# Two rearranged stages of a four-layer decoder kernel: the products of a memory chunk regrouped around their waits, and the quantized network's elementwise work cut into thirds and quarters

## The reference, cut to what matters

```python
# first branch: 4 chunks of 64 tokens, 8 batches, W1 and W2 of 32 x 32 each
for c0 in range(0, S, CHUNK):
    g = _grad_fn(W_state, k[:, sl], v[:, sl]) * GRAD_SCALE
    g = g * jnp.minimum(MAX_GRAD_NORM / gn, 1.0)             # gn: norm of g, per token
    # per token t:  Sm = eta*Sm - theta*g ;  Wm = (1-alpha)*Wm + Sm
    (S_state, W_state), Wtraj = jax.lax.scan(step, (S_state, W_state), xs)
    h = jax.nn.silu(jnp.einsum('btd,btod->bto', q[:, sl], W1t))   # W1t, W2t: the state at token t
    outs.append(jnp.einsum('bto,btpo->btp', h, W2t))
# last branch
def act_qdq(x):
    scale = jnp.maximum(jnp.max(jnp.abs(x)) / qmax, 1e-12)   # one step size for the whole tensor
    return jnp.clip(jnp.round(x / scale), -qmax - 1.0, qmax) * scale
x = act_qdq(x)
up = act_qdq(x @ lpbq_dequant(w_up).T)
gate = act_qdq(x @ lpbq_dequant(w_gate).T)
sig = fixed_qdq_u16(jax.nn.sigmoid(gate))
gate = act_qdq(gate * sig)
o = act_qdq(gate * up)
return o @ lpbq_dequant(w_down).T
```

## Time and profile before

| | us |
|---|---|
| median of three runs (lowest, highest) | 5105.78 (5103.46, 5122.11) |
| profiled execution | 5113.21 |
| its span, first to last instruction | 5111.4 |
| PE busy | 4084.8 (80%) |
| DVE busy | 3495.8 (68%) |
| ACT busy | 2508.5 (49%) |
| POOL busy | 1378.3 (27%) |

### The profile page before, as it was taken

How to read it: one execution, slowest core, us unless ns; L and a number is a source line. 1 busy time by engine, 2 the same in 40 slices (tenths; PEclk the granted TensorE clock), 3 DMA queues, 4 the chain that set the end, 5 groups by cost and what they waited for, 6 DMA issues and landing times. The chain is left out here.

```text
span 5111.4 us, 77588 instructions
## 1 busy us (share of the span) xinstructions
PE 4084.8 (80%) x29250; PEld 2216.5 (43%) x29315; DVE 3495.8 (68%) x5424; ACT 2508.5 (49%) x3542; POOL 1378.3 (27%) x1033
## 2 busy tenths in 40 slices
PE   5740596999999999999995995866995768888872
PEld 3530234666666666666652332432443332222221
DVE  5379444677777777777784445766773648888867
ACT  2120142666666666666662223543563345776762
POOL 0000300566666666666665302000000100000000
PEclk5565698999999999999997997987997788999986
DMA  0010001000000000000003106316540333323200
GB/s 19 1 60 0 0 0 51 1 14 1 14 1 14 14 1 14 1 14 1 1 1 129 58 0 148 54 14 108 81 72 4 95 66 59 55 43 49 47 2 8
DMA packets 135604, 167.70 MB, mean 33 GB/s; under 512 B 19499, under 2 KB 108093, under 8 KB 134677
## 3 DMA queue, kind: packets, MB, share of 16 engines
q1 hardware_dynamic: 127540, 146.39, 14.1%
q0 software_dynamic: 6528, 16.42, 1.3%
q10 hardware_dynamic: 1184, 0.12, 0.0%
HBM read 125.31 MB, written 34.55 MB: 31 GB/s over the span
## 5 line engine op out<-in xcount | busy, mean ns | idle before, releaser
L2992 POOL TENSOR_TENSOR arena<-arena 128x512 f32<-128x512 f32 (+1 forms) x768 | 1131.8, 1475 | 692.2 <-ACT arena L2948 638.8
L2443 ACT ACTIVATE arena<-ps 128x1024 f32<-128x1024 f32 (+1 forms) x688 | 703.9, 1024 | 331.9 <-PE ps L2368 321.4
L2461 DVE TENSOR_REDUCE arena<-ps 128x2 f32<-128x826 f32 (+1 forms) x576 | 565.0, 981 | 183.6 <-PE ps L2314 175.1
L3008 DVE TENSOR_TENSOR arena<-arena 128x1024 f32<-128x1024 f32 (+1 forms) x448 | 645.9, 1480 | 13.8 <-ACT arena L2975 13.8
L3030 DVE TENSOR_TENSOR arena<-ps,arena 128x512 f32<-128x512 f32 (+1 forms) x768 | 530.3, 691 | 177.8 <-ACT arena L2942 144.4
L2314 PE MATMUL ps<-arena 48*128 48x413 bf16 (+3 forms) x1920 | 435.2, 333 | 135.0 <-DVE arena L2461 67.2
L2942 ACT ACTIVATE arena<-ps 128x1024 f32<-128x1024 f32 (+1 forms) x448 | 410.6, 961 | 204.8 <-PE ps L2870 194.3
L2854 PE MATMUL ps<-arena 128*128 128x256 f32 (+1 forms) x1664 | 444.1, 392 | 20.5 <-DVE arena L3016 19.2
L2948 ACT ACTIVATE arena<-arena 128x1024 f32<-128x1024 f32 (+1 forms) x448 | 424.9, 992 | 50.7 <-DVE arena L3008 48.2
L2387 PE MATMUL ps<-arena 128*9 128x256 f32 (+2 forms) x5504 | 435.3, 388 | 11.7 <-ACT arena L2431 8.0
L2870 PE MATMUL ps<-arena 64*128 64x256 f32 (+1 forms) x3328 | 427.3, 391 | 5.6 <-ACT arena L2964 1.3
(11 more groups left out here) (645 smaller groups left out, 5796.0 us busy)
## 6 DMA issues: line engine op xcount, KB each, us to landing
arena<-ctx_parts SPq DMA_DIRECT2D x96, 200.1 KB
arena<-ctx_parts SPq DMA_DIRECT2D x192, 100.1 KB
arena<-in_ctx_feat SPq DMA_DIRECT2D x8, 1601.0 KB, 6.5
arena<-in_ctx SPq DMA_DIRECT2D x16, 768.0 KB
arena<-diff_att_stack SPq DMA_DIRECT2D x60, 192.0 KB
ctx_parts<-arena SPq DMA_DIRECT2D x24, 400.2 KB, 3.7
arena<-in_w SPq DMA_DIRECT2D x1, 6416.0 KB, 18.6
arena<-in_ctx_feat SPq DMA_DIRECT2D x8, 800.5 KB
```

What stands on the lines that cost most here:

```text
L2443: act.activation(self.prob[0:rows, u % 3, :], self.ps[0:rows, 2 * (u % 2):2 * (u % 2) + 2, :].rearrange("p n c -> p (n c)"), ACT.Exp).then ...
L2461: ins = dve.tensor_reduce(dst[:, :, j // 2], self.ps[:, 4:6, 0:hi - lo], AX.X, ALU.max)
L2992: pool.tensor_tensor(acc[0:rows, u % 2, :], before, sc[0:rows, u % 2, t, :], ALU.add).then_inc(added, 1)
L3008: dve.tensor_tensor(e, e, mb[0:rows, u % 2, None, :].to_broadcast([rows, n, 2 * S]), ALU.subtract).then_inc(sub_done, 1)
```

## The change

In a memory chunk, a product of one row of zeros (512 columns, bf16) now opens bank 6 and bank 0: it writes zeros over the whole bank, and all products after it only add. So the eight batches' products with `Wst` and `Sst` no longer have to stand next to the one with `cg`. They are issued ahead of the wait for `cg_ready`, and in the second sum behind a wait for `hA` and `hB` and ahead of the wait for the masked product. The update products move up, from the end of the chunk to just behind the first sum. VectorE's order in a chunk stays the same. A tile `zero` is cleared once.

In the quantized network `gate` is computed ahead of `up`. Magnitudes are taken part by part, each followed by a maximum over three columns. `to_grid` has two passes in place of three (no clipping), and the weights lose their clip. `gate`, the sigmoid, and the passes after it go by thirds of 2048 columns, and the last quantization by quarters of the tokens ([128, 3, 512]), each of which releases a quarter of the down products.

```diff
+            dve.memset(m["zero"][:, :], 0.0)
...
+            def open_bank(n):
+                pe.matmul(ps[0:HM, n, :], m["zero"][:, 0:HM], m["zero"][:, HM:], start=True, stop=False)
+            open_bank(6)
+            for b in range(B):
+                pe.matmul(bank(6)[:, b, :], m["Wst"][:, 0, b, :], qA[:, b, :], start=False, stop=False)
+                pe.matmul(bank(6)[:, b, :], m["Sst"][:, 0, b, :], qB[:, b, :], start=False, stop=False)
             pe.wait_ge(cg_ready, 1)
             for b in range(B):
-                pe.matmul(bank(6)[:, b, :], m["Wst"][:, 0, b, :], qA[:, b, :], start=True, stop=False)
-                pe.matmul(bank(6)[:, b, :], m["Sst"][:, 0, b, :], qB[:, b, :], start=False, stop=False)
-                ins = pe.matmul(bank(6)[:, b, :], cg[:, 1, b, :], GM[:, b, :], start=False, stop=True)
+                ins = pe.matmul(bank(6)[:, b, :], cg[:, 1, b, :], GM[:, b, :], start=False, stop=(b == B - 1))
             ins.then_inc(y_ready, 1)
...
+            pe.wait_ge(hab_ready, 1)
+            open_bank(0)
+            for b in range(B):
+                pe.matmul(bank(0)[:, b, :], m["Wst"][:, 1, b, :], hA[:, b, :], start=False, stop=False)
+                pe.matmul(bank(0)[:, b, :], m["Sst"][:, 1, b, :], hB[:, b, :], start=False, stop=False)
+            pe.wait_ge(gm2_ready, 1)
...
-            tt(hB[:, :, :], h[:, :, :], Bc, ALU.mult)
+            tt(hB[:, :, :], h[:, :, :], Bc, ALU.mult).then_inc(hab_ready, 1)
...
                 for c in range(4):
-                    ins = pe.matmul(ps[:, 4 * (n % 2) + c, :], wT[:, n * P:(n + 1) * P],
+                    k = (n + FT) % (2 * FT)
+                    ins = pe.matmul(ps[:, 4 * (n % 2) + c, :], wT[:, k * P:(k + 1) * P],
                                     xq[:, c * BANK:(c + 1) * BANK], start=True, stop=True)
                 ins.then_inc(s["part_in"], 1)
-            pe.wait_ge(s["o_ready"], 1)
             for t in range(NT):
+                if t % 4 == 0:
+                    pe.wait_ge(s["o_ready"], t // 4 + 1)
...
-            act.wait_ge(s["sig_in"], 1)
-            act.activation(sig[:, :, :], gate[:, :, :], ACT.Sigmoid).then_inc(s["sig_ready"], 1)
+            for f in range(FT):
+                act.wait_ge(s["sig_in"], f + 1)
+                act.activation(sig[:, f, :], gate[:, f, :], ACT.Sigmoid).then_inc(s["sig_ready"], 1)
...
+            def part_magnitude(n, f, t):
+                return dve.tensor_reduce(part_mag[:, n - 1, f:f + 1], t, AX.X, ALU.max, apply_absolute_value=True)
...
+            def to_grid(n, t, out):
+
                 link(ts(out, t, grid[:, 1, n:n + 1], ROUND, ALU.mult, ALU.add))
-                link(ts(out, out, -ROUND, QMAX, ALU.add, ALU.min))
-                link(ts(out, out, -QMAX - 1.0, grid[:, 0, n:n + 1], ALU.max, ALU.mult))
-
-            magnitude(0, x_tok[:, :, :].rearrange("p t d -> p (t d)"), AX.X)
+                return ts(out, out, -ROUND, grid[:, 0, n:n + 1], ALU.add, ALU.mult)
...
-            link(ts(wt[:, :], wt[:, :], 7.0, -8.0, ALU.min, ALU.max))
...
+            for f in range(FT):
+                dve.wait_ge(s["part_out"], f + 1)
+                ins = part_magnitude(1, f, gate[:, f, :])
+            magnitude_of_parts(1, ins)
+            dve.wait_ge(s["part_out"], FT + 1)
+            part_magnitude(2, 0, up[:, 0, :])
+            step_of(1)
+            for f in range(FT):
+                to_grid(1, gate[:, f, :], gate[:, f, :]).then_inc(s["sig_in"], 1)
+            for f in range(1, FT):
+                dve.wait_ge(s["part_out"], FT + f + 1)
+                ins = part_magnitude(2, f, up[:, f, :])
+            magnitude_of_parts(2, ins)
...
+            step_of(2)
             flat = lambda t: t[:, :, :].rearrange("p f t -> p (f t)")
...
+            link(to_grid(2, flat(up), flat(up)))
+            step_of(3)
+            for f in range(FT):
+                link(to_grid(3, gate[:, f, :], gate[:, f, :]))
+                link(tt(up[:, f, :], up[:, f, :], gate[:, f, :], ALU.mult))
+                ins = part_magnitude(4, f, up[:, f, :])
+            magnitude_of_parts(4, ins)
+            step_of(4)
+            for g in range(4):
+                cut = up[:, :, g * BANK:(g + 1) * BANK]
+                to_grid(4, cut, cut).then_inc(s["o_ready"], 1)
```

More of the change, by code:

```diff
@@ L590, in _ @@
                 ins.then_inc(upd_ready, 1)
+            pe.wait_ge(h_ready, 1)
+            for b in range(B):
+                ins = pe.matmul(bank(7, 64)[:, b, :], h0[:, b, :], h[:, b, :], start=True, stop=True)
+            ins.then_inc(g2_ready, 1)
+            pe.wait_ge(hab_ready, 1)
+            open_bank(0)
+            for b in range(B):
+                pe.matmul(bank(0)[:, b, :], m["Wst"][:, 1, b, :], hA[:, b, :], start=False, stop=False)
+                pe.matmul(bank(0)[:, b, :], m["Sst"][:, 1, b, :], hB[:, b, :], start=False, stop=False)
+            pe.wait_ge(gm2_ready, 1)
+            for b in range(B):
+                ins = pe.matmul(bank(0)[:, b, :], cg[:, 0, b, :], GM2[:, b, :], start=False, stop=(b == B - 1))
+            ins.then_inc(out_ready, 1)
         @block.scalar
@@ L747, in stage0 @@
         m["W2"] = st.sb("W2", [HM, B, HM])
+        m["zero"] = st.sb("zero", [1, HM + BANK], BF16)
         memory_inputs(env, m)
@@ L4374, in _ @@
-            dve.wait_ge(s["part_out"], 2 * FT)
-            magnitude(2, gate[:, :, :], AX.XY)
-            flat = lambda t: t[:, :, :].rearrange("p f t -> p (f t)")
-            to_grid(2, flat(gate), flat(gate))
-            dve.sem_inc(s["sig_in"], 1)
-            to_grid(1, flat(up), flat(up))
-            dve.wait_ge(s["sig_ready"], 1)
-            link(ts(flat(sig), flat(sig), 65536.0, ROUND, ALU.mult, ALU.add))
-            link(ts(flat(sig), flat(sig), -ROUND, 65535.0, ALU.add, ALU.min))
@@ L4384, in _ @@
-            link(stt(out=flat(gate), in0=flat(sig), scalar=1.0 / 65536.0, in1=flat(gate), op0=ALU.mult, op1=ALU.mult))
-            magnitude(3, gate[:, :, :], AX.XY)
-            to_grid(3, flat(gate), flat(gate))
-            link(tt(flat(up), flat(up), flat(gate), ALU.mult))
-            magnitude(4, up[:, :, :], AX.XY)
-            to_grid(4, flat(up), flat(up))
-            dve.sem_inc(s["o_ready"], 1)
+            for f in range(FT):
+                dve.wait_ge(s["part_out"], f + 1)
+                ins = part_magnitude(1, f, gate[:, f, :])
@@ new lines, in _ @@
+            magnitude_of_parts(1, ins)
[9 more added lines that the diff above has]
+            for f in range(FT):
+                dve.wait_ge(s["sig_ready"], f + 1)
+                link(ts(sig[:, f, :], sig[:, f, :], 65536.0, ROUND, ALU.mult, ALU.add))
+                link(ts(sig[:, f, :], sig[:, f, :], -ROUND, 65535.0, ALU.add, ALU.min))
+                link(stt(out=gate[:, f, :], in0=sig[:, f, :], scalar=1.0 / 65536.0, in1=gate[:, f, :], op0=ALU.mult,
+                         op1=ALU.mult))
+                ins = part_magnitude(3, f, gate[:, f, :])
@@ new lines, in _ @@
+            magnitude_of_parts(3, ins)
+            step_of(2)
+            flat = lambda t: t[:, :, :].rearrange("p f t -> p (f t)")
+            link(to_grid(2, flat(up), flat(up)))
+            step_of(3)
+            for f in range(FT):
+                link(to_grid(3, gate[:, f, :], gate[:, f, :]))
[3 more added lines that the diff above has]
+            step_of(4)
```

32 lines of the change are left out of this document (13 added, 19 removed).

## The result

The changed kernel takes 5064.43 us, the median of seven runs (5046.86 to 5068.68). The kernel before, run beside it, has a median of 5105.78 us (seven runs, 5088.74 to 5122.23). The ratio over all the runs is 0.9908, with a 95% interval of 0.9890 to 0.9926: 0.9% faster, clear of the noise (the two medians alone would give 0.9919, inside the interval). The profiled execution took 5068.68 us with a span of 5066.8, against 5113.21 and 5111.4.

What follows compares the result with a forecast made beforehand. No engine is busy throughout, so only the chain inside each changed stage counts. Memory chunks 24.3 plus quantized network 21.45 give 45.8 us, taking 5113.21 to 5067.4, or 5060 us from the median; range 5045 to 5079.

Steps and rivals of the forecast that it cites:

- Pitch and change of tile: TensorE's small products in a memory chunk: 0.107 us a record, and 0.13 us more for each change of tile.
- First sum: Memory chunk: only the 16 records with `cg` stay on the chain, so the sum ends 5.36 us earlier.
- Update products in the way: Memory chunks 0 to 2: moved-up update products delay g2, giving back 1.9 us of the first gain.
- Second sum: Memory chunk, to the sum's end: 5.7 us gained in each of chunks 0 to 2, 7.6 in the last.
- Memory chunks as a whole: All four memory chunks: 17.2 + 7.6 - 0.5 for clearing `zero`, 24.3 us gained.
- Quantized network: Last stage: TensorE's down products start 23.1 us earlier, less 1.65 for VectorE's late last group, 21.45 us gained.
- The quarter pass: Last quantization on VectorE: one pass over three runs of 512 columns takes 1.28 us, between 1.02 and 1.75.
- The stages between: Untouched stages between memory chunks and quantized network: a difference above a few microseconds would show the prediction wrong.
- The clock did not rise in the chunks: Rival, memory chunks: denser TensorE work raises the clock to 2.4 GHz, 12 us less, 5048; chance 0.07.
- The gaps did not stay: Rival, both sums: the 0.13 us belongs to accumulating, not the tile; 3 us in each of four chunks, 5072; chance 0.14.
- the quarters were not at the slow rate: Rival, last quantization: quarter passes run at the slow rate, 3.9 us more, 5064, or 5070 with thirds; chance 0.13.
- the clock elsewhere: Rival, stages between: they meet the clock differently; 92 us more at the lower level eats all 45.8 us; chance 0.04.

Runs made afterwards that it cites:

- regroup_only: Changed kernel with update products at the chunk's end and each sum's `Wst` and `Sst` products behind its wait, nothing issued ahead; 5089.41 us, one run.
- quant_only: Kernel before with only the quantized network changed, memory chunks old; ratio 0.9949 to the kernel before, median 5082.23 us.
- whole_last: Changed kernel with the last quantization over the whole tensor again, two passes of 6144 columns and one release; 5059.87 us, one run.
- warm: Changed kernel with update products at the chunk's end and four extra full-size products at the start of each chunk; 5097.21 us, one run.
- even: Changed kernel with each quarter of the last quantization written as two halves of three runs of 256 columns; 5075.11 us, one run.

## Why the prediction was right

The forecast was 5060 us with a range from 5045 to 5079; measured were 5064.4, and 5058.8 if the ratio is applied to the median of before. The mechanism was right. That the number is off by only 4 us is in part luck: the kernel's own seven runs lie 22 us apart, and two terms were picked between wide bounds, as said below. By its steps:

**Pitch and change of tile.** 0.107 us a record and 0.13 us for a change: both hold in chunk 0 of the trace after (0.21 us for two records, 0.34 and 0.35 with a change), and `regroup_only` shows the 1.5 us per sum that follows from them.

**First sum.** 5.36 us earlier predicted, 5.41 measured. The products ahead of the wait end 1.1 us before `cg`; 1.2 were predicted.

**Update products in the way.** 1.9 us given back in each of three chunks predicted; g2 is 1.90 us farther from `h` than before, and taking the products out of the way gives 1.83. It was the one term of the chunk that runs against the change, and it was there.

**Second sum.** 5.7 us a chunk predicted, 5.9 measured (40.93 to 35.04); the opening product took 0.40 where I chose 0.43, the middle of bounds of 0 and 0.85, which was a guess that came out well. In the last chunk, up to its copy, 7.7 us were gained where 7.6 were predicted. Memory chunks as a whole: 24.3 predicted, 24.85 measured in the pair of traces. The 0.5 us for clearing `zero` can't be read off: the chunks start 0.18 us later in the trace of after, but that start differs by over 2 us between traces.

**Quantized network.** 21.45 us predicted, 23.50 measured. Three steps were sized too small. The first is the start, 0.8 us. I left TensorE's cadence as it was and moved everything by 1.85 us; the first product moved by 1.90, but the fourth copy by 2.62. The difference is the moment at which the clock rises, as the windows above show. Seven more kernels have the same code up to that point. Over these eight traces the first copy comes between 5.2 and 6.4 us behind the first product (`quant_only` 6.4, which is 1.1 of its 1.3 us), and the fourth copy starts between 26.8 and 28.2 us into the stage, 27.5 in the mean. The trace of after has it at 26.9, so some 0.6 us of the 23.5 is a draw and not an effect. The second is VectorE's work from the end of the fourth copy to the first pass over a quarter: 67.0 us predicted, 66.4 measured, for the greater part because each pass over a third of the sigmoid took 1.22 to 1.25 us where I took 1.29. The third is in the groups of the end, 0.7 us: VectorE needs 2.40 us for one where I took 2.49 from a row with waits in it, and its first 2.11. I had VectorE start the last group 17.6 us behind the first pass, and it was 16.9. (By the terms it gives, from 5073.5 with three groups of 2.49, the prediction should have had that start 1.9 us behind TensorE and not 1.65, so 21.2 us in place of 21.45.) The quarter pass, the term with the widest bounds (1.02 to 1.75, 1.28 taken), measured 1.28; no row of the trace before could tell.

**The stages between** differ by 3.75 us in the pair of traces, and I had said that more than a few microseconds there would speak against me. Over the eleven traces of this study that stretch, the same code in all, took from 4699.8 us (`whole_last`) to 4726.7 (`warm`), with 4710.9 before and 4714.6 after, and in no order that the edits set. So the 3.75 us can't be told from its own spread, and an effect of the change of a few microseconds there isn't excluded either; one trace of each kernel can't show it. That also is why a total from a single run can't rank two of these kernels: `whole_last` has the shorter span of 5058.1 us, though inside it the network takes 4.2 us more, and `even` has 5073.3 though its network takes 2.1 us less behind the fourth copy.

**The rivals.** The clock did not rise in the chunks, though TensorE was busy without a gap for 11.1 us. The Trainium skill (TensorE: Matmul & The Clock Gate, "What's actually happening") has sustained activity release the clock. The rows differ from that here: the clock stayed at 0.50 with TensorE busy for 11.10 of 11.10 us on products of 32 and 64 rows, while it was 1.00 behind 6.1 us of products of 128 rows in `warm`. The measurement decides. The gaps did not stay, the quarters were not at the slow rate, and the clock elsewhere took nothing that could be told from its own spread.

## What to carry to other kernels

Where several products accumulate into one result and only one of them waits for the long chain, let a cheap product of zeros open the bank and issue the others ahead of the wait; grouping products of one tile shape saves the change of tile as well. Whether the opening product can be left out, with `start=True` on the first of the `Wst` products alone, was not tried; it costs 0.40 us a sum where it stands on the chain. Before moving work up on an engine that runs in order, ask what stands behind it at its new place: the update products had slack to the end of the chunk, and in front of g2 they cost 1.8 us each time. When a tensor is cut so that its consumer can start, write the piece so that its outermost count is even, and look at what the producer owes the consumer's own consumer.

## What the hardware showed that was not expected

- TensorE can be busy without a gap and stay at the lower clock: 11.10 of 11.10 us at 0.50 in a chunk, on products of 32 and 64 rows. In `warm`, after 6.1 us of full-size products the granted clock was 1.00 and a group of 16 small records took 1.07 us. It was 0.50 again from 99 on, behind a gap of 2.00 us, and stayed there through stretches without a gap (3.00 of 3.00 us busy from 114 to 117).
- The same code reaches the upper clock at different moments: from the network's first product to its first copy between 5.2 and 6.4 us in eight traces with the same code up to there.
- A one-input pass on VectorE over three runs of 512 columns took 1.28 us, as much as one over 2048 columns without a break (1.28), and over two by three runs of 256, the same elements, it took 1.02.
